# A graph and attention layer on one core: the self products kept by partition in DRAM instead of by row

## The reference, cut to what matters

```
agg  = segment_sum(xn[dst], src)
gnn  = relu(xn @ self_w.T + self_b + agg @ neigh_w.T + neigh_b)
x    = x + gnn + mix(xn)
x    = x + ffn(layernorm(x))
```

## Time and profile before

| | us |
|---|---|
| median of 3 runs | 3375.29 |
| lowest and highest run | 3372.77 and 3378.03 |
| the profiled execution's own time | 3367.38 |
| its span in the trace | 3365.7 |
| mean granted clock of PE in it | 0.928 of full speed |

### The profile page before, as it was taken

The page is one execution under the profiler, slowest core; times in us unless marked ns, Lnnn a source line. Parts: engine busy times, 40 slices in busy tenths (PEclk is TensorE's granted clock), DMA queues, the critical chain, the costliest instruction groups (busy, mean ns, idle before and its releaser), DMA issues. The chain is left out here.

```text
span 3365.7 us, 49752 instructions
## 1 busy us (share of the span) xinstructions
PE 2853.5 (85%) x11444; PEld 1830.2 (54%) x11445; DVE 2233.7 (66%) x3560; ACT 608.2 (18%) x1075; POOL 2292.9 (68%) x2884
## 2 busy tenths in 40 slices
PE   4869999989788939978888888888887686799898
PEld 1438888745477727753333333333332584587687
DVE  9945555476566537766777777777776568566566
ACT  1013333201111113420000000000000343233233
POOL 0077777688888747747777777777777783565565
PEclk8979999999989969999999999999999556899999
DMA  2314444456566454437777777777778673576464
GB/s 101 131 53 153 153 153 151 154 199 216 188 217 211 161 207 134 130 117 213 218 217 222 220 213 220 222 215 218 219 214 184 214 253 100 174 258 230 161 196 145
DMA packets 283765, 618.95 MB, mean 184 GB/s; under 512 B 57671, under 2 KB 62800, under 8 KB 283625
## 3 DMA queue, kind: packets, MB, share of 16 engines
q0 software_dynamic: 120416, 316.67, 31.7%
q1 hardware_dynamic: 135656, 249.51, 21.8%
q10 hardware_dynamic: 27552, 51.39, 4.2%
HBM read 461.65 MB, written 161.39 MB: 185 GB/s over the span
## 5 line engine op out<-in xcount | busy, mean ns | idle before, releaser
L212 POOL DMA_INDIRECT rec_d<-rec,to x782 | 884.9, 1132 | 229.4 <-issue 227.3
L1626 PE MATMUL PA<-gathered,onehot 128*128 128x512 f32 x1668 | 853.3, 626 | 157.5 <-DMA gathered<-y_d,from 128.8
L1597 POOL DMA_INDIRECT gathered<-y_d,from x834 | 800.8, 960 | 234.3 <-issue 202.8
L1712 DVE TENSOR_TENSOR agg<-agg,PA 128x512 f32 x834 | 571.6, 685 | 255.5 <-PE PA L1626 194.7
L1626 PEld LDWEIGHTS PA<-gathered,onehot 128*128 128x128 f32 x1668 | 273.9, 190 | 673.3 <-DVE agg L1712 375.2
L2426 DVE TENSOR_TENSOR ZLm<-PTZm,ZHm 128x512 fp32r<-128x512 f32 x112 | 77.4, 691 | 151.5 <-ACT ZHm L2404 151.5
L1699 DVE TENSOR_TENSOR onehot<-PC,row_f 128x768 f32<-128x768 f32 x139 | 132.2, 951 | 50.2 <-PE PA L1626 39.9
L2359 PE MATMUL PHm<-e_hi,ZHm 128*128 x448 | 137.8, 307 | 5.1 <-DVE ZLm L2426 4.2
L2323 POOL DMA_INDIRECT ZX<-zx_d,from_m x112 | 109.6, 978 | 28.4 <-issue 19.9
L2359 PE MATMUL PHm<-e_hi,ZLm 128*128 x448 | 126.4, 282 | 0.0
L2359 PE MATMUL PHm<-e_lo,ZHm 128*128 x448 | 126.3, 282 | 0.0
(11 more groups left out here) (448 smaller groups left out, 6769.2 us busy)
## 6 DMA issues: line engine op xcount, KB each, us to landing
Qc<-q_d SPq DMA_DIRECT2D x14, 1792.0 KB, 17.0
Kc<-k_d SPq DMA_DIRECT2D x14, 1792.0 KB, 10.3
gathered<-y_d,from POOLq DMA_INDIRECT x834, 3.7
xn_d<-XN SPq DMA_DIRECT2D x49, 256.0 KB, 3.0
q_d<-Q SPq DMA_DIRECT2D x49, 256.0 KB, 2.0
k_d<-K SPq DMA_DIRECT2D x49, 256.0 KB
v_d<-V SPq DMA_DIRECT2D x49, 256.0 KB, 2.0
XNc<-xn_d ACTq DMA_DIRECT2D x49, 256.0 KB, 6.1
```

The source lines that it names most:

```text
L212: e.indirect_dma_start(dest, bass.IndirectOffsetOnAxis(to[s][0:rows, j:j + 1], 0), rec[s][0:rows, 2 * j:2 * j + 2], None).then_inc(scat.se ...
L1597: e.indirect_dma_start(gathered[s][j][:, :], None, y_d, bass.IndirectOffsetOnAxis(from8[s][:, j:j + 1], 0))\
L1626: e.matmul(PA[j][:, :], onehot[s][:, j, :], gathered[s][j][:, :], start=True, stop=True)\
L1712: e.tensor_tensor(rows, rows, PA[j][:, :], ALU.add).then_inc(f_add.sem, 1)
```

## The change

`self_d` becomes a tensor of 128 partitions by 49 x 512 values, the layout that `agg` has in SBUF. A store now writes its 128 pieces of 2 KB at a distance of 100,352 bytes from each other, where before they lay one behind the other. A load now reads one piece of 14,336 bytes for each partition, 128 in all, where before it read seven pieces of 2 KB for each, 896 in all. Nothing else differs: the same issues on the same queues in the same order, the same bytes.

```diff
-    self_d = dram("self_d", [NP, D])
+    self_d = dram("self_d", [P, TILES * D])
...
                 def store_self(u, b):
                     if not (isinstance(u, int) and u < 0):
                         e.wait_ge(f_so.sem, f_so.after(u))
-                        e.dma_start(tile_rows(self_d, u), SO[b][:, :]).then_inc(self_out.sems[b], 16)
+                        e.dma_start(self_d[:, bass.ds(u * D, D)], SO[b][:, :]).then_inc(self_out.sems[b], 16)
...
                 for i in range(AGG_LOADS):
                     n = TILES // AGG_LOADS
-                    e.dma_start(agg[:, i * n * D:(i + 1) * n * D].rearrange("p (t d) -> p t d", d=D),
-                                self_d[i * n * P:(i + 1) * n * P, :].rearrange("(t p) d -> p t d", p=P))\
+                    e.dma_start(agg[:, i * n * D:(i + 1) * n * D], self_d[:, i * n * D:(i + 1) * n * D])\
                         .then_inc(s_agg, 16)
```

## The result

The changed kernel takes 3388.5 us, the kernel before, run beside it on the same chip, 3374.0: a ratio of 1.0045, 95% interval 1.0034 to 1.0055, that is 11.5 to 18.6 us slower. The forecast was +13.4 us and 3388.7.

The account below looks back on a forecast made before the run. Bound: the block's start, then PE's pace. Full speed from 1196.8, plus 30.1 agg, 3.6 SP, 0.3 POOL, 1.0 tail, 1.0 release: L 1232.8; plus 11.4, first step 1244.2, +13.4. On 3375.3: 3388.7 us, range 3368 to 3393.

Parts of the forecast that it names:

- L: Block start: landing of the nine small weight loads on SP's queue, forecast to move from 1213.24 to 1232.8 us, after agg.
- The chain behind L: From that landing, PE's bias rows (8.8 us), then DVE's copies and hand-over (2.6): PE's first tile step at L + 11.4.
- the low end: Lower end of the forecast's own range: +9 us, with full speed from the first packet, no tail, PE's clock back sooner.
- ACT free by 1198: Block start: ACT's seven agg issues over by some 1198 us, not 1222.56; 6.2 us gained if L stayed at 1213.24.
- The long pieces stay whole: ACT's queue: agg pieces of 14,336 bytes are not cut, each lasting 0.54 us at 427 GB/s.
- rival B: ACT's queue: hardware cuts long pieces into parts of some 3.6 KB; L = 1219, change comes out at nothing; chance 0.15.
- Rival A: Block start: engines' turns go by bytes, small loads keep their share; -13.9 us, or -6.2 with L as today; chance 0.13.
- rival C: Block writing self products: the changed stores slow enough for DVE to wait for its buffer, adding to the loss; chance 0.02.
- Late next: After the nine: SP's first tile loads land with them, 11 us before use; POOL's delayed scatters covered by its 28.8 us wait.
- The shift reaches the block's end undiminished: The block runs at PE's pace (46.4 of 50 us busy), so its first step's shift reaches the kernel's end whole.

Follow-up runs that it names:

- E2: Changed kernel with the aggregate read in loads of two tiles, pieces of 4 KB, in place of seven long loads; ratio to the kernel before 1.0005.
- E3: Changed kernel with the nine weight loads issued at the head of ACT's queue, ahead of the seven agg loads, not on SP's; ratio to the kernel before 0.9980.
- E5: Kernel before (2 KB pieces, rows contiguous) with its seven agg loads issued by ACT after its weight activations; ratio to the kernel before 1.0008.
- E1: Changed kernel, stores kept, with the aggregate read by 49 loads of one tile, pieces of 2 KB; ratio to the kernel before 1.0006.
- E4: Changed kernel with the seven long agg loads written after ACT's seven weight activations in place of before them; ratio to the kernel before 0.9988.
- E9: E4 with SP issuing two tiles' loads behind the nine weight loads, ACT waiting for them, and 14 agg loads of 7,168 bytes per partition; ratio to before 0.9963.
- E10: Changed kernel with agg read in 28 loads of 3,584 bytes per partition, one per tile step, issued on ACT behind high_u; ratio to the kernel before 1.0095.

## Why the prediction was right

- *L is the end of everything.* Forecast 1232.8, found 1231.9, in a block that began 0.3 us later. The counts and E2 tie it to the turns: L follows the length of the piece, at equal numbers of packets. In E3, with the nine ahead in the same queue, the long pieces hold them up no more.
- *The chain behind L.* Forecast 11.4 us, found 11.1 (1231.89 to 1243.01): PE's bias rows took 8.4 us in place of 8.8, at a mean granted clock of 0.53 against 0.50, its lower level. What the low end allowed for, a clock that comes back sooner after the shorter idle time, does not show: from 1244 to 1250 it was 0.50 again, and it rose some 7 us after the first step, as before.
- *ACT free by 1198.* Found 1198.4. True, and worth nothing alone; E5's wait of 22.2 us shows the issue time on the path once the landing is early.
- *The long pieces stay whole, at 0.54 us each.* 896 of them are counted; rival B is out for this length. Its arithmetic for parts of some 4 KB held when the program cut them itself (E2).
- *Rival A,* turns by bytes, is out by 351 to 350.
- *Stores, rival C:* nothing, as taken (E1).
- *Late next:* nothing, as taken. DVE's first step on a tile's load (L1447) follows the bias rows without a wait, and its waits on XNe are 4.7 us in all against 6.6.
- *The shift reaches the block's end undiminished:* 11.8 us at the first step and 10.2 at the end, counted from the block's start, so 1.7 were recovered. This held here and is no rule: E4 has a first step 16.5 us earlier and ends the block where the kernel before does. The block's pace depends on how its tile loads meet others.

The mechanism is borne out. That the sum hit 13.4 against a measured 14.5 is closer than its bounds deserve, and in part luck: the traces, one execution of each kernel, show 10.2 us in the block, and the rest is not shown to come from the change.

## What to carry to other kernels

Before lengthening the pieces of a transfer, look for the small loads that run beside it on another queue and count their pieces: here the two queues sent equal numbers, so each small piece cost the time of a long one, and a transfer that nobody waits for can hold up one that everybody waits for. If such loads exist, order them ahead (the same queue, or a wait), and only then use long pieces; here E9, with pieces of half the length, turned a loss of 0.45% into a gain of 0.37%. A transfer spread into a loop must be placed against the transfer that the loop waits for, and its place in time is checked in the timeline, not in the program.

## What the runs showed of the hardware that was not expected

- A DMA issue on ACT does not wait for the activations that stand before it in the program. In E4 the seven issues began at 1200.93, 0.02 us after the first of the seven activations they were written behind; the other six began from 1201.33 to 1203.16. In E10 the issue began at 1347.32, 0.2 us after the table load of the activation before it, and 1.1 us ahead of that activation itself.
- With long pieces on ACT's queue SP's issues themselves got slow, 7.23 us for the load of a single row at 1198.18 where it took 0.96 us before. By their shapes the three loads ahead of it had put 80 pieces per engine on SP's queue; on ACT's queue before, 145 entries per engine were open when its seven issues ended (4066 of 6384 packets had moved by then). No cost shows, as the counts of the two queues stay equal while these issues drag on. What held them was not tried and stays open; so does E9's arrangement in the layout by row.
